# One kernel, a stack of eight gated attention and feed-forward blocks: TensorE's order, its PSUM banks and its idle stretches rearranged

## The chip, the cores and the metric

One core of a Trainium2 chip runs the whole program. The metric is the device time of one execution in microseconds, from the first to the last instruction and what lies around them; lower is better. TensorE (PE) multiplies, VectorE (DVE), ScalarE (ACT) and GpSimd (POOL) do the rest, SyncE (SP) issues the transfers.

## What is computed

The input is x of 64 batches x 64 tokens x 128 features and a context of 64 x 64 x 256. Eight blocks follow one another, each on a layer norm of x and each added to x with a gate:

```python
x = x + tanh(g_xattn[0]) * cross_attention(ctx, norm(x), masks)          # l0a: 8 heads of 16
x = x + tanh(g_ffn[0])   * two_layers(norm(x))                           # l0f0, l0f1: local attention, 8 heads of 64, and a gated MLP
x = x + tanh(g_xattn[1]) * (norm(x) @ W_in + b_in + patches of ctx)      # l1a
x = x + tanh(g_ffn[1])   * top2_of_8_experts(norm(x))                    # l1f
x = x + tanh(g_xattn[2]) * attention(norm(x), ctx, mask)                 # l2a: 8 heads of 16
x = x + tanh(g_ffn[2])   * ternary_mlp(norm(x))                          # l2f, l2g
x = x + tanh(g_xattn[3]) * attention(norm(x), [ctx, x])                  # l3a: 16 heads of 8, 128 keys, halves l3a0 and l3a1
x = x + tanh(g_ffn[3])   * ternary_conv_mlp(norm(x))                     # l3f, l3g
```

All of it is float32, with the masks and biases as bfloat16 rows that are multiplied by rows of ones (a value is split into three such rows).

## The kernel before

The 4,096 tokens are 32 tiles of 128 tokens (two batches). A tile goes through all eight blocks; nothing passes between tiles. Each engine runs one stream of instructions, written out by `in_turn`: every piece of work of a tile is a stage with a name (`l0f0_qk` is the multiplication for queries and keys in the first layer of block l0f), a table per engine gives each stage a time, tile i's stages are moved by i times `PERIOD`, and the engine's stream is all stages in order of that time. The numbers set nothing but the order. Five tiles (G = 5 sets of buffers) are under way at once, so each engine alternates between the stages of five tiles, and in the steady part the same sequence repeats once per tile: one turn of the sequence is called a period here.

Stages wait for one another with semaphores. In TensorE's chain `tile(name)` waits until stage `name` of the same tile is done (the operands), and `take(name)` waits until the readers of the PSUM banks that the stage writes are done with what stood there before. `BANK_TABLE` gives every TensorE stage its first bank, how many banks it takes, and which stage reads it last. TensorE works through its stream in order: whatever stands behind a waiting instruction waits too. Before, a stage first waits for its operands, then takes its banks, and then multiplies, masks and biases first:

```python
yield f"{n}_sc"                      # L1407
tile(f"{n}_qts")
take(f"{n}_sc")
...
mm(pair_of_banks(f"{n}_sc", 256)[:, h2], ident_bf[:], bc(causal[:], 1, 4), start=True, stop=False)
```

The stages of which the prediction speaks, in TensorE's stream: `l0f0_qk`, `l0f1_qk` (L1392, 128x512), `l0f0_v`, `l0f1_v` (L1398), `l0f0_qkt` and `l0f1_qkt` (L1405, eight transposes), `l0f0_sc` and `l0f1_sc` (L1412 the causal mask, L1418 the scores), `l1f_lg` (L1517, L1518), `l2a_yt` (a transpose, L1325), `l2a_sc` (L1346 and L1349 the mask and the logit bias, L1354 the scores), `l3a0_sc` and `l3a1_sc` (L1575), `l3f_hid` (L1619, the convolution; its start is used as the mark of a period). Around them: DVE's maximum and subtraction of a softmax (`_max` L1013, `_sub` L1016), its rotation of queries and keys (`_turned` L1067 and L1070) and their scaling (`_qkn` L1076), its `_y` (L997, the normalised tile), ACT's copies out of PSUM (L743), and POOL's powers (L507).

Of the kernel before, what the change touches and what calls it, by code (L numbers as in the profile page):

```python
# [42 lines left out]
PE_TIMES = """
    l0a_kv 711, l0a_yt 780, l0a_q 834, l0a_sc 855, l0a_pt 907, l0a_pv 914, l0a_ot 931, l0a_out 940, l0f0_yt 1016,
    l0f0_qk 1030, l0f0_v 1149, l0f0_qkt 1163, l0f0_sc 1163, l0f0_pt 1243, l0f0_pv 1303, l0f0_ot 1359, l0f0_wo 1379,
    l0f0_sh 1401, l0f0_lt 1465, l0f0_hid 1495, l0f0_out 1548, l0f1_yt 1573, l0f1_qk 1609, l0f1_v 1629,
    l0f1_qkt 1720, l0f1_sc 1819, l0f1_pt 1860, l0f1_pv 1879, l0f1_ot 1889, l0f1_wo 1897, l0f1_sh 1917, l0f1_lt 1977,
    l0f1_hid 1995, l0f1_out 2035, l1a_yt 2058, l1a_out 2065, l1f_yt 2102, l1f_lg 2102, l1f_ot 2188, l1f_out 2196,
    l2a_yt 2247, l2a_sc 2268, l2a_pt 2321, l2a_pv 2344, l2f_qt 2399, l2f_hid 2431, l2g_qt 2494, l2g_out 2520,
    l3a_yt 2539, l3a_qkv 2545, l3a0_sc 2564, l3a1_sc 2658, l3a0_pt 2693, l3a0_pv 2706, l3a1_pt 2712, l3a1_pv 2760,  # L50
    l3a_tt 2791, l3a_ot 2852, l3a_out 2863, l3f_qt 2896, l3f_hid 2941, l3g_qt 3022, l3g_out 3029
    """
# [12 lines left out]
DVE_TIMES = """
    l0a_st 652, l0a_var 667, l0a_eps 673, l0a_y 812, l0a_k 818, l0a_qs 838, l0a_max 868, l0a_sub 872, l0a_inv 947,
    l0a_o 953, l0a_x 973, l0f_st 976, l0f_var 990, l0f_eps 996, l0f_y 1000, l0f0_den 1105, l0f0_turned 1115,
    l0f0_qkn 1193, l0f0_max 1264, l0f0_sub 1286, l0f0_inv 1327, l0f0_o 1327, l0f0_y1 1385, l0f0_st 1405,
    l0f0_var 1425, l0f0_eps 1447, l0f0_y 1461, l0f0_gated 1526, l0f0_x 1571, l0f1_den 1695, l0f1_turned 1709,
    l0f1_qkn 1778, l0f1_max 1817, l0f1_sub 1839, l0f1_inv 1885, l0f1_o 1885, l0f1_y1 1943, l0f1_st 1951,  # L70
    l0f1_var 1951, l0f1_eps 1954, l0f1_y 1962, l0f1_gated 2039, l0f1_x 2054, l1a_st 2054, l1a_var 2054,
    l1a_eps 2068, l1a_y 2088, l1a_x 2106, l1f_st 2126, l1f_var 2127, l1f_eps 2139, l1f_lgs 2175, l1f_top 2196,
    l1f_mid 2202, l1f_rest 2218, l1f_sel 2218, l1f_w 2235, l1f_o 2248, l1f_x 2271, l2a_st 2278, l2a_var 2278,
    l2a_eps 2278, l2a_y 2278, l2a_max 2303, l2a_sub 2305, l2a_inv 2345, l2a_o 2362, l2a_x 2362, l2f_st 2362,
    l2f_var 2362, l2f_eps 2362, l2f_y 2362, l2f_abs 2377, l2f_lim 2411, l2f_inv 2419, l2f_step 2431, l2f_pre 2446,
    l2g_abs 2471, l2g_lim 2473, l2g_inv 2480, l2g_step 2480, l2g_x 2539, l3a_st 2539, l3a_var 2540, l3a_eps 2543,
    l3a_y 2550, l3a_part 2583, l3a0_max 2627, l3a0_sub 2644, l3a1_max 2752, l3a1_sub 2760, l3a_inv 2796, l3a_o 2821,
    l3a_x 2865, l3f_st 2865, l3f_var 2869, l3f_eps 2883, l3f_y 2883, l3f_abs 2908, l3f_lim 2910, l3f_inv 2917,
    l3f_step 2917, l3f_q 2923, l3f_act 2970, l3g_abs 2970, l3g_lim 2970, l3g_inv 3000, l3g_step 3024, l3f_x 3082
    """  # L80
# [1651 lines left out]
```

## Time and profile before

| | us |
|---|---|
| median of 3 runs | 1748.58 |
| lowest, highest | 1740.39, 1751.47 |
| the profiled execution, its own time | 1760.33 |
| its span | 1758.6 |
| TensorE busy | 1474.8 (84%) |
| VectorE busy | 1367.9 (78%) |
| ScalarE busy | 965.0 (55%) |
| GpSimd busy | 743.2 (42%) |
| mean granted TensorE clock | 0.911 of full |

Full TensorE clock is 2.4 GHz, granted clock 0.5 is 1.2 GHz. The share of an engine is a mean over a start, a steady part of some 1,335 us in which five tiles are under way, and an end in which the pipeline empties.

### The profile page before, as it was taken

Reading aid. Unit: us, or ns where it says so; the run is one execution under the profiler, and the core shown is the slowest. Engines: PE = TensorE matmul, PEld = TensorE weight load, DVE = VectorE, ACT = ScalarE, POOL = GpSimd, SP = SyncE. Lnnn points to the kernel's source line nnn. Section 1 sums busy time; section 2 is a strip of 40 time slices with the busy share of each in tenths; the row PEclk is TensorE's granted clock in tenths of the full one; section 3 lists DMA queues with packets and bytes.
Section 4 is the critical chain, followed back from the end, with each engine's and each line's share of the span. In section 5 each row is a group of like instructions: output and inputs, shape, how many; then the busy total and the mean of one; then the engine's idle time right before and its main releaser. Section 6 shows DMA issues by size and latency. Waiting matters only on the chain.

```text
span 1758.6 us, 42092 instructions
## 1 busy us (share of the span) xinstructions
PE 1474.8 (84%) x16270; PEld 1005.9 (57%) x16270; DVE 1367.9 (78%) x4054; ACT 965.0 (55%) x1992; POOL 743.2 (42%) x1143
## 2 busy tenths in 40 slices
PE   2567888899888889999888889998988889988764
PEld 1445565666566555666656566666566566665432
DVE  3356788887888888888888889888788888887652
ACT  1134565666566665666665565566555556565432
POOL 4244454433444554433544454444444554442200
PEclk9688899998999998999999999999899999998875
DMA  6001110111111110111111111011111110111100
GB/s 205 4 8 27 39 40 15 39 41 41 29 41 41 40 40 16 39 41 41 41 29 41 40 40 29 26 41 41 41 29 40 40 40 17 28 31 30 27 23 3
DMA packets 130948, 64.36 MB, mean 37 GB/s; under 512 B 97591, under 2 KB 123575, under 8 KB 130494
## 3 DMA queue, kind: packets, MB, share of 16 engines
q1 hardware_dynamic: 130750, 61.66, 13.5%
q8 instruction: 131, 2.15, 0.5%
q14 instruction: 67, 0.55, 0.1%
HBM read 50.05 MB, written 2.14 MB: 30 GB/s over the span
## 4 chain that ended last, share of the span: by engine, by line
PE 35%; DVE 35%; ACT 13%; POOL 8%; issue 7%; POOLq 2%; DVEq 0%
PE ps_all L1619 5%; DVE mx L1013 3%; POOL rden L507 3%; PE ps_all L1392 3%; PE ps_all L1575 3%; DVE wide_b L1016 3%; ACT wide_a L743 3%; DVE wide_b L1070 3%; POOL wide_a L507 3%; PE ps_all L1332 3%; DVE wide_a L1105 2%; DVE wide_a L1067 2%; PE ps_all L1418 2%; DVE den L1061 2%; DVE stats L982 2%
## 5 line engine op out<-in xcount | busy, mean ns | idle before, releaser
L507 POOL TENSOR_TENSOR rstd<-rstd,minus_half 128x1 f32<-128x1 f32 x320 | 177.1, 554 | 815.4 <-DVE rstd L991 815.4
L1013 DVE TENSOR_REDUCE mx<-ps_all 128x8 f32<-128x1024 f32 (+1 forms) x192 | 166.4, 867 | 133.0 <-PE ps_all L1354 96.6
L1332 PE MATMUL ps_all<-ident,wide_b 128*128 128x128 f32 x1024 | 173.8, 303 | 23.1 <-ACT wide_b L756 15.1
L507 POOL TENSOR_TENSOR rden<-rden,minus_half 128x16 f32<-128x16 f32 x64 | 187.6, 2931 | 9.4
L507 POOL TENSOR_TENSOR wide_a<-wide_a,wide_b 128x256 f32<-128x256 f32 x256 | 177.4, 725 | 0.0
L743 ACT COPY wide_a<-ps_all 128x512 f32<-128x512 f32 (+1 forms) x192 | 136.4, 729 | 61.3 <-PE ps_all L1332 36.9
L1332 PEld LDWEIGHTS ps_all<-ident,wide_b 128*128 128x128 f32 x1024 | 124.7, 153 | 53.2 <-ACT wide_b L756 18.4
L1392 PE MATMUL ps_all<-w_qkv,ht_shift 128*128 128x512 f32 x256 | 150.0, 717 | 2.2 <-ACT ht_shift L766 2.2
L743 ACT COPY ht<-ps_all 128x128 f32<-128x128 f32 x160 | 42.9, 268 | 193.1 <-PE ps_all L1325 193.0
L756 ACT ACTIVATE wide_b<-wide_b 128x512 f32<-128x512 f32 (+1 forms) x160 | 114.7, 717 | 44.2 <-DVE wide_b L1016 43.8
L743 ACT COPY wide_c<-ps_all 128x512 f32<-128x512 f32 (+1 forms) x96 | 69.9, 728 | 113.0 <-PE ps_all L1332 111.4
L1016 DVE TENSOR_TENSOR wide_b<-ps_all,mx 128x512 f32<-128x512 f32 (+1 forms) x160 | 125.8, 786 | 2.4
L706 ACT ACT_TABLE_LOAD x70 | 89.8, 1283 | 44.8 <-DVE wide_b L1016 19.4
L1575 PE MATMUL ps_all<-wide_a,qt 32*64 32x512 f32 x512 | 75.1, 668 | 40.0 <-DVE wide_a L1227 39.3
L1450 PE MATMUL ps_all<-ht,w 128*128 128x128 f32 x768 | 98.7, 282 | 1.3 <-ACT ht L741 1.3
L1450 PEld LDWEIGHTS ps_all<-ht,w 128*128 128x128 f32 x768 | 96.4, 201 | 1.8 <-issue 1.8
L1619 PE MATMUL ps_all<-w_conv,xt 128*64 128x512 f32 x384 | 95.1, 633 | 0.0
L1405 PEld LDWEIGHTS ps_all<-ident,wide_b 128*128 128x128 f32 x512 | 69.9, 161 | 40.3 <-issue 40.3
L1405 PE MATMUL ps_all<-ident,wide_b 128*128 128x128 f32 x512 | 78.2, 304 | 15.9 <-DVE wide_b L1076 14.2
L1392 PEld LDWEIGHTS ps_all<-w_qkv,ht_shift 128*128 128x128 f32 x256 | 49.7, 215 | 67.3 <-issue 67.3
L1076 DVE TENSOR_TENSOR wide_b<-wide_a,rden 128x1024 f32<-128x1024 f32 x64 | 77.8, 1215 | 11.3 <-POOL wide_c L675 8.5
L1061 DVE TENSOR_REDUCE den<-wide_c 128x16 f32<-128x1024 f32 x64 | 77.4, 1210 | 5.7 <-ACT wide_c L771 5.6
(267 smaller groups left out, 3714.5 us busy)
## 6 DMA issues: line engine op xcount, KB each, us to landing
wide_a<-in_k SPq DMA_DIRECT2D x64, 256.0 KB, 3.1
wide_c<-wide_c SPq DMA_DIRECT2D x128, 64.0 KB, 2.2
v_pad<-in_v SPq DMA_DIRECT2D x32, 256.0 KB, 3.8
v_pair<-in_v SPq DMA_DIRECT2D x32, 136.0 KB, 2.7
ctx_t<-in_ctx_t SPq DMA_DIRECT2D x32, 128.0 KB, 2.7
ctx_s<-in_ctx SPq DMA_DIRECT2D x32, 128.0 KB, 3.2
xin<-in_x SPq DMA_DIRECT2D x32, 64.0 KB, 2.6
mask_row<-in_mask_f SPq DMA_DIRECT2D x32, 64.0 KB, 3.0
```

The costliest lines, as they stand in the source:

```text
L507: return gp.tensor_tensor(o, a, b, op)
L743: a.copy(to, of).then_inc(*done(name))
L756: a.activation(of[:, s, 0:width], of[:, s, 0:width], ACT.Exp, scale=scale).then_inc(*done(f"{n}_exp"))
L1013: v.tensor_reduce(most, of, AX.X, ALU.max).then_inc(*done(f"{n}_max"))
L1016: tt(to, of, bc(most, 3, of.shape[3]), ALU.subtract).then_inc(*done(f"{n}_sub"))
L1061: v.tensor_reduce(den[:, s, :], wide_c[:, s, 0:2 * BANK].rearrange("p (g e) -> p g e", g=16), AX.X, ALU.add).then_inc(*done(f"{n}_den"))
L1332: m = nc.tensor.transpose(ps(name, c * P, P), of[:, c * P:c * P + P], ident[:])
L1392: m = mm(ps(f"{n}_qk", q * BANK, BANK), hs, w_qkv[:, L, q * INNER:q * INNER + INNER], start=True, stop=True)
L1405: m = nc.tensor.transpose(ps(f"{n}_qkt", c * P, P), wide_b[:, s, c * P:c * P + P], ident[:])
L1450: m = mm(ps(f"{n}_hid", half * BANK + c * P, P), w_1[:, L, half, c, :], ht[:, s, :], start=True, stop=True)
L1575: n_mm = mm(ps_all[64 * b:64 * b + 64, bank + m, :], qt[r, s, 64 * b:64 * b + 64], k_part[r, s, b * BANK:b * BANK + BANK], start=True, sto ...
L1619: m = mm(ps_all[64 * b:64 * b + 64, BANKS["l3f_hid"][0], :], xt[:, s, b, tap:tap + ROW], w_conv[:, tap, :], start=False, stop=(tap == 2))
```

## The change

Four things are changed, three of them on TensorE.

1. In every TensorE stage `take` comes ahead of the wait for operands, and where a stage begins with a mask or a bias, these multiplications come ahead of that wait too (`masks64` is split off from `scores64`; likewise the causal mask of `l0f0_sc` and `l0f1_sc`, and the biases of `l0f0_out`, `l0f1_out`, `l0a_kv`, `l1a_out`, `l3f_hid`).
2. After `take`, nine stages multiply the identity by itself into their own bank, one to three times, 16 times per tile (`WARM`); the stage then overwrites the result.
3. All tables of times and `PERIOD` have new numbers, that is, the streams of all engines are in a new order.
4. `BANK_TABLE` gives most stages other banks.

```diff
-PERIOD = 489
+PERIOD = 464
...
+WARM = {"l0a_yt": 2, "l0f0_qkt": 3, "l0f0_sc": 3, "l0f1_yt": 2, "l1a_yt": 1, "l1a_out": 1, "l1f_out": 1, "l3a_yt": 1, "l3a1_sc": 2}
...
 l0f0_sc 6 2 l0f0_sub
...
-l0f1_qk 6 2 l0f1_turned
+l0f1_qk 0 2 l0f1_turned
...
                         held[k] = [(reader, i) for reader in readers]
 
+                    for _ in range(WARM.get(name, 0)):
+                        mm(ps(name, 0, P), ident[:], ident[:], start=True, stop=True)
...
                     yield name
+                    take(name)
                     tile(wait)
-                    take(name)
                     nc.tensor.transpose(ps(name, 0, P), of, ident[:]).then_inc(*done(name))
...
                     yield f"{n}_sc"
-                    tile(f"{n}_qts")
                     take(f"{n}_sc")
                     settle(pe, "pe_waits")
                     for h2 in range(2):
                         mm(pair_of_banks(f"{n}_sc", 256)[:, h2], ident_bf[:], bc(causal[:], 1, 4), start=True, stop=False)
+                    tile(f"{n}_qts")
+                    settle(pe, "pe_waits")
...
                 yield "l2a_sc"
+                masks64("l2a", 1)
                 tile("l2a_ht")
                 pe.wait_ge(signal(f"second_in{s}"), loaded(i, 32))
-                take("l2a_sc")
-                settle(pe, "pe_waits")
-                scores64("l2a", ht[:, s, :], k_part[:, s, 0:BANK], 1)
+                scores64("l2a", ht[:, s, :], k_part[:, s, 0:BANK])
```

The first place is TensorE's stream around the queries and keys of the two layers of l0f, in the steady part. Before, in order: `l0f1_qk`, `l1f_yt`, `l1f_lg`, `l0f1_v` and `l0f0_v` (of two tiles), `l0f0_qkt`, `l0f0_sc`, `l3a1_sc`, and then the first stage of a new tile, `l0a_kv`:

```order
L1392 MATMUL ps_all<-w_qkv,ht_shift 128x512 x2
L1325 MATMUL ps_all<-ident,x 128x128
L1517 MATMUL ps_all<-w_gate,ht 128x8
L1518 MATMUL ps_all<-w_a,ht 128x128
L1398 MATMUL ps_all<-w_qkv,ht_shift 128x512 x2
L1405 MATMUL ps_all<-ident,wide_b 128x128 x8
L1412 MATMUL ps_all<-causal,ident_bf 128x256 x2
L1418 MATMUL ps_all<-wide_a 64x64 x16
L1575 MATMUL ps_all<-wide_a,qt 64x512 x4
L1465 MATMUL ps_all<-rows,row_sel 128x128
L1467 MATMUL ps_all<-w_src,ctx_t 128x128 x2
```

In the changed kernel the same stretch is `l0f1_qk`, `l1f_yt`, `l0f0_v`, `l1f_lg`, `l0f0_qkt`, `l0f0_sc`, `l3a1_sc`:

```order
L1403 MATMUL ps_all<-w_qkv,ht_shift 128x512 x2
L1329 MATMUL ps_all<-ident,x 128x128
L1409 MATMUL ps_all<-w_qkv,ht_shift 128x512
L1527 MATMUL ps_all<-w_gate,ht 128x8
L1528 MATMUL ps_all<-w_a,ht 128x128
L1319 MATMUL ps_all<-ident 128x128 x3
L1416 MATMUL ps_all<-ident,wide_b 128x128 x8
L1319 MATMUL ps_all<-ident 128x128 x3
L1422 MATMUL ps_all<-causal,ident_bf 128x256 x2
L1430 MATMUL ps_all<-wide_a 64x64 x16
L1319 MATMUL ps_all<-ident 128x128 x2
L1584 MATMUL ps_all<-wide_a,qt 64x512 x4
```

One of the two value multiplications stands ahead of `l1f_lg`, the other one has gone behind `l0a_kv` (its row is not in the piece); three identity multiplications stand ahead of the eight transposes, three ahead of the causal mask, and two ahead of `l3a1_sc`.

The second place is DVE's stream around the scores of l2a. Before, it is `l1f_x`, the statistics of l2a (L982, L985, L991), `l2a_y`, `l0a_y`, `l0a_k`, `l2a_max`, `l2a_sub`, `l0f0_inv`, `l0f0_o`, `l0a_qs`:

```order
L1190 TENSOR_TENSOR x<-ps_all,x 128x128
L982 BN_STATS stats<-x 128x6
L985 BN_AGGR mv<-stats 128x2
L991 TENSOR_SCALAR rstd<-mv 128x1
L997 TENSOR_SCALAR y<-x,mv,rstd 128x128
L997 TENSOR_SCALAR y<-xin,mv,rstd 128x128
L1132 SCALAR_TENSOR_TENSOR ot<-ps_all,b_k,mask_row 128x128
L1013 TENSOR_REDUCE mx<-ps_all 128x8
L1016 TENSOR_TENSOR wide_b<-ps_all,mx 128x512
L1024 RECIPROCAL rden<-ps_all 128x8
L1027 TENSOR_TENSOR wide_b<-ps_all,rden 128x2x4x64
L1136 SCALAR_TENSOR_TENSOR qt<-ps_all,b_q,mask_row 128x128
```

In the changed kernel the same names stand in this order, with all lines one further down in the file:

```order
L1191 TENSOR_TENSOR x<-ps_all,x 128x128
L983 BN_STATS stats<-x 128x6
L986 BN_AGGR mv<-stats 128x2
L992 TENSOR_SCALAR rstd<-mv 128x1
L1133 SCALAR_TENSOR_TENSOR ot<-ps_all,b_k,mask_row 128x128
L998 TENSOR_SCALAR y<-x,mv,rstd 128x128
L1137 SCALAR_TENSOR_TENSOR qt<-ps_all,b_q,mask_row 128x128
L1014 TENSOR_REDUCE mx<-ps_all 128x8
L1017 TENSOR_TENSOR wide_b<-ps_all,mx 128x512
L1014 TENSOR_REDUCE mx<-ps_all 128x8
L1017 TENSOR_TENSOR wide_b<-ps_all,mx 128x2x4x64
L1025 RECIPROCAL rden<-ps_all 128x8
```

`l0a_y` is gone from here (it stands some 20 stages earlier), `l0a_k` stands ahead of `l2a_y`, `l0a_qs` behind it and ahead of `l2a_max`, and `l0f1_max` and `l0f1_sub` follow at once on those of l2a.

The third piece is TensorE's stream at the same place. Before, four mask and bias rows follow `l0a_yt` and `l2a_yt`:

```order
L1325 MATMUL ps_all<-ident,y 128x128 x2
L1346 MATMUL ps_all<-rows,row_sel 128x256
L1349 MATMUL ps_all<-rows,row_sel 128x256
L1346 MATMUL ps_all<-rows,row_sel 128x256
L1349 MATMUL ps_all<-rows,row_sel 128x256
L1354 MATMUL ps_all<-wide_a,ht 64x256 x4
L1593 MATMUL ps_all<-wide_b,v_pad 32x64 x16
L1366 MATMUL ps_all<-wide_c,wide_a 64x65 x16
L1475 MATMUL ps_all<-ht,w_tgt 128x128
```

In the changed kernel only one transpose is left ahead of them, `l0a_q` stands between, and the scores of `l0f1_sc` follow before the values of l3a1 (L1602) and l0f0 (L1377):

```order
L1329 MATMUL ps_all<-ident,y 128x128
L1486 MATMUL ps_all<-ht,w_tgt 128x128
L1351 MATMUL ps_all<-rows,row_sel 128x256
L1354 MATMUL ps_all<-rows,row_sel 128x256
L1351 MATMUL ps_all<-rows,row_sel 128x256
L1354 MATMUL ps_all<-rows,row_sel 128x256
L1365 MATMUL ps_all<-wide_a,ht 64x256 x4
L1422 MATMUL ps_all<-causal,ident_bf 128x256 x2
L1430 MATMUL ps_all<-wide_a 64x64 x16
L1602 MATMUL ps_all<-wide_b,v_pad 32x64 x16
L1377 MATMUL ps_all<-wide_c,wide_a 64x65 x16
```

The order of the four mask rows and the scores is the same in both; what moved is the wait for `l2a_ht`, from ahead of the mask rows to behind them.

## Rows read from the trace of the kernel before

**Rows 1.** Windows: busy us (instructions) of each engine, granted clock, DMA share, GB/s.
```profile
core 0: us, PE busy (x) PEld busy (x) DVE busy (x) ACT busy (x) POOL busy (x), PEclk, DMA share, GB/s
0.00:229.40 229.40, 143.01 (x1379) 102.13 (x1379) 131.07 (x358) 76.78 (x159) 93.58 (x169) 0.85 0.19 54
229.40:1564.10 1334.70, 1196.59 (x13717) 822.34 (x13716) 1126.32 (x3376) 803.46 (x1675) 612.99 (x918) 0.94 0.14 36
1564.10:1758.60 194.50, 135.22 (x1176) 81.46 (x1175) 110.55 (x323) 84.78 (x160) 36.67 (x56) 0.77 0.08 22
```

**Rows 2.** The page's chain that ended last, shares of the span.
```profile
PE 35%; DVE 35%; ACT 13%; POOL 8%; issue 7%; POOLq 2%; DVEq 0%
```

**Rows 3.** Timeline of PE: the convolution, which marks a period (start, duration).
```profile
872.16 2.80 PE L1619 MATMUL ps_all<-w_conv,xt 128*64 128x512 f32 x12
...
919.48 2.79 PE L1619 MATMUL ps_all<-w_conv,xt 128*64 128x512 f32 x12
...
969.12 2.79 PE L1619 MATMUL ps_all<-w_conv,xt 128*64 128x512 f32 x12
```

**Rows 4.** Windows of two successive periods, columns as in rows 1.
```profile
871.50:918.82 47.32, 41.90 (x510) 28.94 (x509) 41.64 (x126) 29.84 (x62) 22.67 (x34) 1.00 0.14 38
918.82:968.46 49.64, 44.57 (x510) 31.45 (x509) 41.65 (x126) 29.72 (x62) 22.68 (x34) 0.93 0.15 36
```

**Rows 5.** Timeline of PE in a full-clock stretch: start, us, what, [idle before <-releaser].
```profile
887.29 1.09 PE L1575 MATMUL ps_all<-wide_a,qt 32*64 32x512 f32 x8 [1.32 <-DVE wide_a L1227]
...
891.06 0.36 PE L1517 MATMUL ps_all<-w_gate,ht 128*128 128x8 f32 x2 [0.66 <-DVE wide_b L1016]
...
891.58 1.88 PE L1398 MATMUL ps_all<-w_qkv,ht_shift 128*128 128x512 f32 x4
893.30 1.04 PE L1405 MATMUL ps_all<-ident,wide_b 128*128 128x128 f32 x8
895.81 0.38 PE L1412 MATMUL ps_all<-causal,ident_bf 128*128 128x256 bf16 x2 [1.47 <-DVE wide_b L1070]
896.12 0.69 PE L1418 MATMUL ps_all<-wide_a 64*64 64x64 f32 x32
896.74 1.09 PE L1575 MATMUL ps_all<-wide_a,qt 32*64 32x512 f32 x8
...
899.77 1.09 PE L1332 MATMUL ps_all<-ident,wide_b 128*128 128x128 f32 x8
```

**Rows 6.** Timeline of PE one period on, at half clock.
```profile
948.62 1.91 PE L1332 MATMUL ps_all<-ident,wide_b 128*128 128x128 f32 x8
```

**Rows 7.** Timelines of DVE and ACT beside rows 5.
```profile
890.84 1.22 DVE L1076 TENSOR_TENSOR wide_b<-wide_a,rden 128x1024 f32<-128x1024 f32 x1
...
894.38 1.01 ACT L743 COPY wide_a<-ps_all 128x1024 f32<-128x1024 f32 x1 [0.28 <-PE ps_all L1405]
...
894.43 1.27 DVE L1070 TENSOR_TENSOR wide_b<-ps_all,turn 128x512 f32<-128x512 f32 x2
```

**Rows 8.** Timeline of DVE around the scores of l2a.
```profile
901.90 0.28 DVE L1190 TENSOR_TENSOR x<-ps_all,x 128x128 f32<-128x128 f32 x1
...
903.58 0.35 DVE L997 TENSOR_SCALAR y<-x,mv,rstd 128x128 f32<-128x128 f32 x1 [0.67 <-POOL rstd L507]
...
904.10 0.35 DVE L1132 SCALAR_TENSOR_TENSOR ot<-ps_all,b_k,mask_row 128x128 f32<-128x128 f32 x1
906.33 0.69 DVE L1013 TENSOR_REDUCE mx<-ps_all 128x8 f32<-128x512 f32 x1 [1.89 <-PE ps_all L1354]
```

**Rows 9.** Timeline of PE at the same place.
```profile
903.40 1.06 PE L1332 MATMUL ps_all<-ident,wide_a 128*128 128x128 f32 x8
904.32 0.41 PE L1325 MATMUL ps_all<-ident,y 128*128 128x128 f32 x2
905.08 0.27 PE L1346 MATMUL ps_all<-rows,row_sel 128*128 128x256 bf16 x1 [0.35 <-ACT ht L741]
...
905.60 0.66 PE L1354 MATMUL ps_all<-wide_a,ht 64*64 64x256 f32 x8
```

**Rows 10.** Timeline of PE: six 128x128 float32 multiplications (12 records) and what follows.
```profile
922.37 1.50 PE L1450 MATMUL ps_all<-ht,w 128*128 128x128 f32 x12
923.71 0.27 PE L1325 MATMUL ps_all<-ident,y 128*128 128x128 f32 x1
```

More of the change, by code:

```diff
@@ L39 @@
 BIASES = 1408
-PERIOD = 489
+PERIOD = 464
 PE_TIMES = """
[L44 to L51, printed above, removed]
+    l0a_kv 180, l0a_yt 211, l0a_q 253, l0a_sc 300, l0a_pt 375, l0a_pv 378, l0a_ot 394, l0a_out 395, l0f0_yt 470,
+    l0f0_qk 494, l0f0_v 601, l0f0_qkt 625, l0f0_sc 625, l0f0_pt 699, l0f0_pv 725, l0f0_ot 810, l0f0_wo 833,
+    l0f0_sh 841, l0f0_lt 870, l0f0_hid 931, l0f0_out 985, l0f1_yt 986, l0f1_qk 1061, l0f1_v 1123, l0f1_qkt 1158,
+    l0f1_sc 1183, l0f1_pt 1257, l0f1_pv 1287, l0f1_ot 1304, l0f1_wo 1314, l0f1_sh 1329, l0f1_lt 1358, l0f1_hid 1407,
+    l0f1_out 1449, l1a_yt 1477, l1a_out 1489, l1f_yt 1526, l1f_lg 1544, l1f_ot 1595, l1f_out 1614, l2a_yt 1632,
+    l2a_sc 1646, l2a_pt 1682, l2a_pv 1695, l2f_qt 1787, l2f_hid 1810, l2g_qt 1876, l2g_out 1906, l3a_yt 1941,
+    l3a_qkv 1944, l3a0_sc 1977, l3a1_sc 2019, l3a0_pt 2063, l3a0_pv 2079, l3a1_pt 2092, l3a1_pv 2114, l3a_tt 2122,
+    l3a_ot 2179, l3a_out 2189, l3f_qt 2259, l3f_hid 2285, l3g_qt 2380, l3g_out 2409
@@ L76 @@
[L76 to L79, printed above, removed]
+    l0a_st 89, l0a_var 105, l0a_eps 135, l0a_y 168, l0a_k 282, l0a_qs 284, l0a_max 315, l0a_sub 322, l0a_inv 361,
@@ L96 @@
     """
 BANK_TABLE = """
-l0a_kv 3 1 l0a_k
+l0a_kv 0 1 l0a_k
 l0a_yt 7 1 l0a_ht
-l0a_q 4 1 l0a_qs
-l0a_sc 0 2 l0a_sub
-l0a_pt 1 1 l0a_pts
-l0a_pv 4 2 l0a_o
+l0a_q 3 1 l0a_qs
+l0a_sc 2 2 l0a_sub
+l0a_pt 7 1 l0a_pts
+l0a_pv 5 2 l0a_o
 l0a_ot 1 1 l0a_ots
-l0a_out 5 1 l0a_x
+l0a_out 3 1 l0a_x
 l0f0_yt 5 1 l0f0_hs
-l0f0_qk 4 2 l0f0_turned
-l0f0_v 0 1 l0f0_vs
-l0f0_qkt 1 2 l0f0_qts
+l0f0_qk 3 2 l0f0_turned
+l0f0_v 7 1 l0f0_vs
+l0f0_qkt 3 2 l0f0_qts
 l0f0_sc 6 2 l0f0_sub
-l0f0_pt 2 1 l0f0_pts
-l0f0_pv 1 2 l0f0_o
@@ L128 @@
-l0f1_sh 0 1 l0f1_y
-l0f1_lt 4 1 l0f1_lts
-l0f1_hid 1 2 l0f1_gated
-l0f1_out 6 1 l0f1_x
-l1a_yt 0 1 l1a_ht
-l1a_out 1 1 l1a_x
-l1f_yt 2 1 l1f_ht
-l1f_lg 4 1 l1f_o
-l1f_ot 4 1 l1f_ots
-l1f_out 0 1 l1f_x
-l2a_yt 4 1 l2a_ht
-l2a_sc 5 2 l2a_sub
-l2a_pt 5 1 l2a_pts
-l2a_pv 6 2 l2a_o
-l2f_qt 5 1 l2f_qts
-l2f_hid 2 1 l2f_pre
-l2g_qt 0 1 l2g_qts
-l2g_out 7 1 l2g_x
-l3a_yt 3 1 l3a_ht
-l3a_qkv 6 2 l3a_part l3a_vs
+l0f1_sc 2 2 l0f1_sub
+l0f1_pt 0 1 l0f1_pts
+l0f1_pv 2 2 l0f1_o
+l0f1_ot 1 1 l0f1_ots
+l0f1_wo 7 1 l0f1_y1
@@ L148 @@
+l0f1_sh 4 1 l0f1_y
+l0f1_lt 4 1 l0f1_lts
+l0f1_hid 0 2 l0f1_gated
+l0f1_out 7 1 l0f1_x
+l1a_yt 5 1 l1a_ht
+l1a_out 6 1 l1a_x
+l1f_yt 6 1 l1f_ht
+l1f_lg 5 1 l1f_o
+l1f_ot 5 1 l1f_ots
+l1f_out 6 1 l1f_x
+l2a_yt 7 1 l2a_ht
+l2a_sc 4 2 l2a_sub
+l2a_pt 4 1 l2a_pts
+l2a_pv 5 2 l2a_o
+l2f_qt 5 1 l2f_qts
+l2f_hid 7 1 l2f_pre
+l2g_qt 2 1 l2g_qts
+l2g_out 6 1 l2g_x
+l3a_yt 7 1 l3a_ht
+l3a_qkv 0 2 l3a_part l3a_vs
 l3a0_sc 3 2 l3a0_sub
-l3a1_sc 1 2 l3a1_sub
-l3a0_pt 6 2 l3a0_pts
-l3a0_pv 0 1 l3a0_os
+l3a1_sc 2 2 l3a1_sub
@@ L1384, in layer @@
                     yield f"{n}_qk"
+                    take(f"{n}_qk")
                     tile(f"{n}_hs")
@@ L1423, in layer @@
                     yield f"{n}_pv"
+                    take(f"{n}_pv")
                     tile(f"{n}_pts")
@@ L1514, in chain @@
                 yield "l1f_lg"
+                take("l1f_lg")
                 tile("l1f_ht")
-                take("l1f_lg")
                 mm(ps("l1f_lg", P, E), ht[:, s, :], w_gate[:], start=True, stop=True)
```

154 lines of the change are left out of this document (78 added, 76 removed).

## The prediction, made blind

> **What bounds the kernel now.** I read the windows first. In the steady part TensorE is busy 1196.6 of 1334.7 us and DVE 1126.3, no other engine over 804, at a mean granted clock of 0.94 [rows 1]; the chain of work that ended last lies on PE and DVE for 35% each [rows 2]. So neither alone is the bound: each waits for the other at some places, and the length of a period is what counts. From 229.4 to 1564.1 us there are 27 periods, marked by the start of the convolution: 1334.7 / 27 = 49.43 us each.
>
> Then the marks themselves. The period that starts at 872.16 lasts 47.32 us, the next one 49.64 [rows 3]. Their work is the same, 510 PE records and DVE 41.6 us in both, but the first one has full clock (1.00, 2.4 GHz) and PE busy 41.90, the second one 0.93 and 44.57 [rows 4]. The half clock of 1.2 GHz doubles what it touches: eight transposes take 1.09 us at full clock and 1.91 at half [rows 5, 6]. So the 2.67 us that PE loses to the clock in the second period show in the period as 2.32. A mean period is 49.43 - 47.32 = 2.11 us longer than one at full clock, 57 us over 27 periods. I take this as the first thing that the change can win.
>
> Where does the clock fall? Ahead of both places PE is idle or in short pieces. In the full-clock stretch PE waits 1.32 us ahead of `l3a0_sc`, 0.66 ahead of `l1f_lg`, 1.47 ahead of `l0f0_sc` [rows 5]; one period later the same sequence is at half clock some 4 us behind that last wait [rows 6]. In all PE is idle 47.32 - 41.90 = 5.42 us of a full-clock period, DVE 47.32 - 41.64 = 5.68 [rows 4].
>
> The Trainium skill ("TensorE: Matmul & The Clock Gate", Part 1) says that for modelling the warm-up costs less than 1% of a typical kernel span, which would be under 18 us here. The trace disagrees: 2.11 of 49.43 us is 4.3%, because the clock falls again in nearly every period. The measurement decides.
>
> **The identity multiplications.** They are 16 per tile. The nearest row is six float32 multiplications of the same size, from 922.37 to 923.71: 1.34 / 6 = 0.223 us each at full clock [rows 10]. So 16 x 0.223 = 3.6 us per period, 7.1 if all ran at half clock. The trace before shows none, so from both sides: at best they lie wholly in PE's idle time and lift the clock for good, which is worth 2.11 us; at worst they lie on the path and lift nothing, which costs 3.6 to 4. PE's own floor becomes 41.9 + 3.6 = 45.5 us. They stand at just the places named: five in the stages ahead of `l3a0_sc` (`l0f1_yt`, `l3a_yt`, `l1a_yt`, `l1a_out`), eight from `l0f0_qkt` to `l3a1_sc`, three close behind. I take it that they win back four fifths of the 2.11, and leave 0.4: they turn idle time into activity right ahead of the points where the clock fell, but PE will still wait somewhere.
>
> The skill's page on TensorE ("TensorE: Matmul & The Clock Gate", Part 4) says that transposes do not engage the full clock as multiplications do. The two stretches ahead of the falls do hold many transposes, and the added ones are plain multiplications; no row here separates the two kinds. It would change my 0.4 to about 0.
>
> **The order and the masks, at full clock.** First place, the queries and keys of l0f0. DVE has scaled them at 890.84 + 1.22 = 892.06 [rows 7], but PE gets to the transposes only at 893.30, behind `l1f_lg` and two value multiplications in 1.88 us [rows 5]. With one of the two gone from there (1.88 / 2, near 0.9), PE is free near 891.6; three identities (0.67) take it to 892.3. The transposes start 1.0 us earlier. ACT's copy (1.01 us, 894.38 before [rows 7]) then ends near 894.4. Before, the scores also waited for banks 6 and 7, which DVE read for the other layer until 894.43 + 1.27 = 895.70 [rows 7]; `l0f1_qk` now has banks 0 and 1, so that wait goes. Three identities and the causal mask (0.67 + 0.3) lie beside ACT's copy. The scores start near 894.4 against 896.12 [rows 5], 1.7 us earlier. What is late next is DVE: it has the 41.6 us to do, runs without a gap here, and the maximum of these scores still stands behind the rotation of the other layer. So at this place PE gains 1.7 us less the 0.45 of the two identities ahead of `l3a1_sc`, and the path gains nothing by itself; the gain is that PE is early at the next place.
>
> Second place, the scores of l2a. Here DVE is the one that waits: `l1f_x` at 901.90, 0.67 us of idle for POOL's power, `l2a_y` at 903.58, `l0a_k` at 904.10, and then 1.89 us idle until the scores of l2a let it start at 906.33 [rows 8]. On PE that chain is: `l2a_yt` at 904.32, held up by eight transposes of l3a1 until then, 0.35 us for ACT's copy, four mask rows from 905.08 to 905.60, scores from 905.60 [rows 9]. After the change PE arrives here about 1 us earlier, so the transpose can follow `l2a_y` (near 903.95), the copy ends near 904.6, and the masks (905.60 - 905.08 = 0.52 us) lie inside the wait for it. Scores start near 904.65, and DVE near 905.35: 1.0 us sooner. DVE moreover does `l0a_qs` (an operation like the 0.35 of `l0a_k`) inside what is left of the 1.89, work that had stood behind it. Against that, `l0a_y` (another 0.35) has left this stretch, where it cost nothing, for the dense part ahead of `l1f_x`. `l0a_k` was beside the wait and still is. Sum at this place: 1.0 + 0.35 - 0.35 = 1.0 us.
>
> The mask rows of the other stages, the biases ahead of their operands and the extra semaphore pieces (three more per tile) I cost at nothing: they lie beside waits for operands that PE has there anyway, and the semaphores beside the multiplications still under way. If that cover is not there, each mask row that the path loses or keeps is 0.13 us (0.52 / 4 [rows 9]), a few tenths in all, either way. The other reordering, ACT's and POOL's too, I cannot price from rows; both have room (29.8 and 22.7 busy of 47.3 [rows 4]). Bounds: nothing from below, and from above all of DVE's idle time, to its floor of 41.6. I take nothing.
>
> So at full clock: by DVE's path 47.32 - 1.0 = 46.3; by PE, 45.5 of work and some wait that nothing fills, half of the 1.32 ahead of `l3a0_sc` at least, 46.2. I take 46.3, plus 0.4 for what is left of the slow clock: **46.7 us a period.**
>
> **The sum.** 27 x (49.43 - 46.7) = 73.7 us. The start and the end (229.4 and 194.5 us at clocks of 0.85 and 0.77 [rows 1]) have far more idle time than the steady part; more clock there, at 0 to 15 us, of which I take 5, as the waits are longer than one to three multiplications can bridge. That is 78.7 us off the profiled execution's own 1760.33, 1681.6. The median of the runs shown lies 11.75 below it, 1748.58, so **1670 us**.
>
> **Rivals.**
> - *PE becomes the bound, and the clock is whole* (10%). All waits fill, the period is 45.6: 27 x 3.83 + 8 = 111 us less, 1637. For it: every other engine has 4 us to spare. Against: PE and DVE take turns, and neither was ever without waits.
> - *Half of the clock's loss stays* (18%). Whether it falls depends on where the waits come, and the new order has its own. 46.3 + 1.05 = 47.35: 56 + 4 us less, 1689; with less from the order up to 1725.
> - *The identities do not do what they are for* (12%). PE's busy time was 1196.6 / 27 = 44.3 us per period, slow time included. With 16 x 0.25 more (0.25, as an eighth of the time is at half clock, 1 - 0.94 = 0.06, twice) it is 48.3; add 1 us of waits and it is 49.3, no better than 49.43: 1742.
> - *Slower* (8%): the eight identities from `l0f0_qkt` to `l3a1_sc` stand ahead of operands that are there already. This decides itself at one point: if PE reaches `l0f0_qkt` later than DVE's 892.06 plus the time of three identities, each one is on the path. Before, PE was 1.2 us late there. With the clock unchanged, 8 x 0.25 = 2.0 less the 1.0 of the second place, 1.0 x 32 = 32 us more: 1781. Against it: with 0.9 us of value work and the 1.47 us wait gone, it has the time.
>
> **How the numbers follow.** My forecast of 46.7, give or take 0.6 (1654 to 1686), has 52%. Faster by over 1% (below 1731) are the forecast and the first two: 80%. Within 1%, about what this measurement can tell, 12%; slower by over 1%, 8%. The range goes from the first rival's 1637 to the third one's 1742, and leaves out the slower case and a little at either end.
>
> **What would show it.** Marks of the convolution 46 to 47.5 us apart; granted clock of the steady part 0.98 or more against 0.94; PE busy near 45.5 us a period; DVE's wait at L1014 for l2a under 1.0 us against 1.89; the wait ahead of the causal mask gone. Wrong it is if the clock stays at 0.94 (then the identities do not count), or if the clock is whole but the period stays at 47.3 or more (then the order gave nothing, or the identities stand on the path; DVE's idle time would tell).

## The result, and the profile after

The changed kernel takes 1685.4 us (median of 4, 1683.4 to 1686.0), the kernel before beside it on the same chip 1750.0: a ratio of 0.964, 95% interval 0.960 to 0.968. The forecast was 1670 and faster; it is faster, inside the range, and the gain is 65 us where 79 were forecast. Of the two profiled executions, from which the forecast was worked out, the gain is 75.1 us: 1760.33 against 1685.26.

The windows of the changed kernel, with the same columns as [rows 1], give two successive periods and the whole steady part, from the first mark (the convolution, now L1628) to the 28th:

```profile
794.15:841.23 47.08, 44.66 (x542) 32.75 (x543) 41.62 (x126) 29.98 (x63) 23.00 (x34) 1.00 0.15 38
841.23:888.31 47.08, 44.66 (x542) 32.74 (x542) 41.61 (x126) 29.97 (x63) 23.00 (x34) 1.00 0.15 38
222.40:1502.40 1280.00, 1207.36 (x14555) 885.33 (x14582) 1125.86 (x3376) 809.48 (x1675) 620.83 (x918) 1.00 0.15 37
```

Against [rows 1] and [rows 4]: the granted clock is 1.00 in the whole steady part, not 0.94. TensorE is busy 44.7 us of a full-clock period instead of 41.9, with 32 more records (16 float32 multiplications of two each). 27 periods last 1280.0 us, 47.41 each, where they were 49.43; 14 of them last 47.1, the longest four 48.1 to 49.2. The start is 7.0 us shorter (222.4 against 229.4) and what lies behind the 28th mark 13.3 (1683.5 - 1502.4 = 181.1 against 194.4). So the 75.1 us of the two profiled spans are 54.7 in the steady part and 20.4 at the ends.

The chain that ended last has changed hands, to be set beside [rows 2]; POOL was 8% and is now 24%:

```profile
PE 25%; POOL 24%; DVE 20%; issue 11%; ACT 9%; POOLq 7%; SPq 2%; DMA 0%; DVEq 0%
```

TensorE's timeline at the first place, which answers to [rows 5]:

```profile
809.11 1.09 PE L1584 MATMUL ps_all<-wide_a,qt 32*64 32x512 f32 x8 [0.44 <-DVE wide_a L1228]
...
813.37 0.83 PE L1319 MATMUL ps_all<-ident 128*128 128x128 f32 x6
814.03 1.05 PE L1416 MATMUL ps_all<-ident,wide_b 128*128 128x128 f32 x8
814.92 0.83 PE L1319 MATMUL ps_all<-ident 128*128 128x128 f32 x6
815.59 0.38 PE L1422 MATMUL ps_all<-causal,ident_bf 128*128 128x256 bf16 x2
816.28 0.69 PE L1430 MATMUL ps_all<-wide_a 64*64 64x64 f32 x32 [0.31 <-ACT wide_a L744]
```

The waits of 1.32, 0.66 and 1.47 us are now 0.44, none and 0.31. From the start of `l3a0_sc` to that of the scores of `l0f0_sc` it is 7.17 us (816.28 - 809.11); before it was 8.83 (896.12 - 887.29). That is the 1.7 us of the forecast, identities and all.

DVE's and POOL's timelines at the second place answer to [rows 8]; ahead of them stands the mark from which this period is counted:

```profile
794.10 2.79 PE L1628 MATMUL ps_all<-w_conv,xt 128*64 128x512 f32 x12
```

```profile
823.54 0.28 DVE L1191 TENSOR_TENSOR x<-ps_all,x 128x128 f32<-128x128 f32 x1
...
825.87 0.63 DVE L998 TENSOR_SCALAR y<-x,mv,rstd 128x128 f32<-128x128 f32 x1 [1.05 <-POOL rstd L508]
827.20 0.35 DVE L1137 SCALAR_TENSOR_TENSOR qt<-ps_all,b_q,mask_row 128x128 f32<-128x128 f32 x1 [0.71 <-PE ps_all L1486]
828.26 0.69 DVE L1014 TENSOR_REDUCE mx<-ps_all 128x8 f32<-128x512 f32 x1 [0.71 <-PE ps_all L1365]
```

```profile
822.42 1.61 POOL L508 TENSOR_TENSOR ctx_rms<-ctx_rms,minus_half 128x1 f32<-128x1 f32 x1
824.22 0.59 POOL L618 TENSOR_SCALAR far<-plug,patch_row,ctx_rms 128x64 f32<-128x64 f32 x1 [0.18 <-issue]
824.80 0.51 POOL L620 TENSOR_SCALAR far<-plug,patch_row 128x64 f32<-128x64 f32 x1
825.27 0.57 POOL L508 TENSOR_TENSOR rstd<-rstd,minus_half 128x1 f32<-128x1 f32 x1
```

The wait of 1.89 us for the scores has become 0.71 and 0.71, with `l0a_qs` between. But the wait ahead of `l2a_y` has grown from 0.67 to 1.05: POOL's power for it starts at 825.27, behind `pick_reach` of a later tile (L508 `ctx_rms`, L618, L620). From `l1f_x` to `l2a_y` it is 2.33 us now and was 1.68; from `l2a_y` to the maximum 2.39 and was 2.75. In sum DVE gets to the maximum of l2a no sooner: it starts 34.16 us behind the mark of its period (828.26 - 794.10), and before it was 34.17 (906.33 - 872.16). The 0.24 us by which the clean period has become shorter lie behind this maximum, where `l0a_qs` (0.35 us) no longer stands.

### The profile page after: what moved, and what is told of

Its sections match the earlier page's. It is cut to its first block, busy times and chain, and to the rows that moved or that the text cites. A ratio compares the mean times of both kernels' runs of the same rounds, so it can differ in the third digit from the quotient of the medians.

```text
span 1683.5 us, 44176 instructions
## 1 busy us (share of the span) xinstructions
PE 1484.5 (88%) x17261; PEld 1079.7 (64%) x17294; DVE 1366.6 (81%) x4054; ACT 971.6 (58%) x1992; POOL 751.7 (45%) x1143
## 4 chain that ended last, share of the span: by engine, by line
PE 25%; POOL 24%; DVE 20%; issue 11%; ACT 9%; POOLq 7%; SPq 2%; DMA 0%; DVEq 0%
POOL rden L508 9%; POOL wide_a L508 9%; POOL rstd L508 4%; PE ps_all L1336 4%; POOLq L617 3%; POOLq L615 3%; PE ps_all L1377 3%; DVE wide_a L1106 3%; PE ps_all L1329 2%; PE ps_all L1448 2%; ACT L707 2%; PE ps_all L1365 2%; DVE small L1041 2%; DVE y L998 2%; ACT wide_b L788 2%
## 5 line engine op out<-in xcount | busy, mean ns | idle before, releaser
L508 POOL TENSOR_TENSOR rstd<-rstd,minus_half 128x1 f32<-128x1 f32 x320 | 179.0, 565 | 750.7 <-DVE rstd L992 750.6
L508 POOL TENSOR_TENSOR rden<-rden,minus_half 128x16 f32<-128x16 f32 x64 | 187.6, 2931 | 9.4
L508 POOL TENSOR_TENSOR wide_a<-wide_a,wide_b 128x256 f32<-128x256 f32 x256 | 177.6, 724 | 0.0
L1319 PE MATMUL ps_all<-ident 128*128 128x128 f32 x1024 | 167.3, 285 | 7.0 <-DVE wide_b L1017 3.9
L1336 PE MATMUL ps_all<-ident,wide_b 128*128 128x128 f32 x1024 | 149.8, 280 | 26.2 <-ACT wide_b L757 13.0
L744 ACT COPY wide_a<-ps_all 128x512 f32<-128x512 f32 (+1 forms) x192 | 139.7, 729 | 41.1 <-PE ps_all L1336 21.9
L1336 PEld LDWEIGHTS ps_all<-ident,wide_b 128*128 128x128 f32 x1024 | 117.6, 143 | 52.3 <-ACT ht L744 28.6
L1319 PEld LDWEIGHTS ps_all<-ident 128*128 128x128 f32 x1024 | 140.9, 196 | 14.0 <-DVE wide_b L1017 6.3
L1403 PE MATMUL ps_all<-w_qkv,ht_shift 128*128 128x512 f32 x256 | 125.7, 614 | 2.2 <-ACT ht_shift L767 2.2
L1628 PE MATMUL ps_all<-w_conv,xt 128*64 128x512 f32 x384 | 93.4, 623 | 0.4 <-ACT xt L744 0.4
L998 DVE TENSOR_SCALAR y<-x,mv,rstd 128x128 f32<-128x128 f32 x128 | 57.2, 447 | 35.9 <-POOL rstd L508 35.9
L1416 PE MATMUL ps_all<-ident,wide_b 128*128 128x128 f32 x512 | 71.1, 284 | 14.5 <-DVE wide_b L1077 14.5
```

The costliest lines, as they stand in the source:

```text
L508: return gp.tensor_tensor(o, a, b, op)
L744: a.copy(to, of).then_inc(*done(name))
L998: ts(y[:, s, :], x[:, s, :] if of is None else of, mv[:, s, 0:1], rstd[:, s:s + 1], ALU.subtract, ALU.mult).then_inc(*done(f"{n}_y"))
L1319: mm(ps(name, 0, P), ident[:], ident[:], start=True, stop=True)
L1336: m = nc.tensor.transpose(ps(name, c * P, P), of[:, c * P:c * P + P], ident[:])
L1403: m = mm(ps(f"{n}_qk", q * BANK, BANK), hs, w_qkv[:, L, q * INNER:q * INNER + INNER], start=True, stop=True)
```

## The experiments

The runs were timed in three groups, each on one chip beside the kernel before, which had 1750.2, 1753.8 and 1749.6 us in them. The mean period is that over 27 periods between the marks, the clean period the one that most periods of that kernel have at full clock, slow time that at 1.2 GHz per steady period. Periods, clocks and slow times are those of one profiled execution of each kernel. The kernel before has only three periods at full clock, all of 47.32, and old_order_new_waits six.

| kernel | median us | ratio (95%) | mean period | clean period | slow time |
|---|---|---|---|---|---|
| before | | 1 | 49.43 | 47.32 | 5.7 |
| changed | 1685.4 | 0.964 (0.960 to 0.968) | 47.41 | 47.08 | 0 |
| no_warm | 1692.9 | 0.967 (0.962 to 0.971) | 47.61 | 47.07 | 1.5 |
| old_order_new_waits | 1746.6 | 0.997 (0.993 to 1.001) | 49.51 | 47.39 | 5.8 |
| old_order_new_waits_warm | 1731.6 | 0.988 (0.984 to 0.993) | 48.88 | 48.87 | 0 |
| late_masks | 1691.7 | 0.966 (0.962 to 0.970) | 47.59 | 47.50 | 0 |
| new_order_old_waits | 1715.5 | 0.979 (0.976 to 0.982) | 48.16 | 47.52 | 1.1 |
| new_order_old_banks | 2013.9 | 1.149 (1.145 to 1.153) | 58.02 | | 10.2 |
| warm_transposes | 1681.8 | 0.960 (0.958 to 0.962) | 47.40 | 47.08 | 0 |
| pick_moved | 1666.6 | 0.951 (0.948 to 0.954) | 46.86 | 46.55 | 0 |
| dup_first | 1681.7 | 0.960 (0.957 to 0.964) | 47.29 | 47.07 | 0 |
| all_three | 1660.7 | 0.949 (0.946 to 0.952) | 46.71 | 46.42 | 0.1 |
| old_order_transposes | 1706.2 | 0.974 (0.971 to 0.978) | 48.08 | 48.05 | 0 |
| warm_twice | 1717.2 | 0.981 (0.978 to 0.984) | 48.51 | 48.39 | 0 |

**1. The changed kernel without the identities (no_warm).** Theory A, the forecast's, was that they hold up the clock and that this is the gain.

```diff
-WARM = {"l0a_yt": 2, "l0f0_qkt": 3, "l0f0_sc": 3, "l0f1_yt": 2, "l1a_yt": 1, "l1a_out": 1, "l1f_out": 1, "l3a_yt": 1, "l3a1_sc": 2}
+WARM = {}
```

> The changed kernel without its 16 identity multiplications per tile; all else as changed. Theory A (the gain is the clock, and the identities hold it up): the granted clock of the steady part falls back to 0.94 to 0.96, the period grows from 47.4 to 49 or more, 1735 to 1750 us. Rival B (the new order alone has closed the waits, and the identities are ballast on TensorE): the clock stays at 0.98 or more, TensorE has 2.8 us less to do per period, 1665 to 1685 us.

Measured 1692.9 us, 7.5 above the changed kernel, with intervals of the ratio that overlap. Neither expectation was met whole: the time is near Rival B's, but the clock does fall. Two neighbouring periods of it, in the columns of [rows 1]:

```profile
696.10:744.10 48.00, 42.49 (x508) 30.16 (x508) 41.70 (x126) 29.90 (x63) 23.01 (x34) 0.96 0.15 37
744.10:791.20 47.10, 41.13 (x510) 29.06 (x510) 41.64 (x126) 29.96 (x63) 23.01 (x34) 1.00 0.15 38
```

In 12 of the 27 periods the clock falls once and costs mostly some 0.9 us; slow time is 1.5 us a period against 5.7 before. So the new order without any identity already keeps most of the clock, and theory A falls in its size. TensorE is less busy than before (41.13), idle nearly 6 us of 47.1, and its clock still falls less often. So the amount of idle time does not decide it. What differs is how the idle time lies: the longest waits of the clean period are below one microsecond, where [rows 5] has 1.32 and 1.47. That this is the reason is read from the traces; no run changed the length of a wait alone.

```profile
756.15 0.33 PE L1329 MATMUL ps_all<-ident,y 128*128 128x128 f32 x1 [0.85 <-DVE y L998]
759.12 1.09 PE L1584 MATMUL ps_all<-wide_a,qt 32*64 32x512 f32 x8 [0.72 <-DVE wide_a L1228]
...
766.24 0.70 PE L1430 MATMUL ps_all<-wide_a 64*64 64x64 f32 x32 [0.97 <-ACT wide_a L744]
```

**2. Old order and banks, new waits (old_order_new_waits).** The changed kernel's code, with `PERIOD`, the tables of times and `BANK_TABLE` of the kernel before, and `WARM = {}`.

> The kernel before with its own order and banks, but with banks taken and masks and biases multiplied ahead of the operands' wait; no identities. Theory A: the clock stays near 0.94 in the steady part, and the masks alone are worth at most 0.5 us a period: 1735 to 1752 us. Rival B (the masks ahead of the wait fill the idle stretches and so lift the clock): clock 0.97 or more, 1700 us or less.

Measured 1746.6 us, not to be told from the kernel before. Theory A's expectation holds: taking banks and multiplying masks and biases ahead of the wait brings nothing that the times show in the old order (its ten runs go from 1730.6 to 1759.6 us, and its full-clock periods are 47.39 us against 47.32).

**3. The same with the identities (old_order_new_waits_warm).** Only `WARM` is put back.

> The same with the 16 identities per tile: old order and banks, new waits, identities. Theory A: the clock goes to 1.00 in the steady part and the period to 47 to 48 us, 1685 to 1710 us, so that nearly the whole gain is there without the new tables. Rival C (order and banks bring a good part): 1715 to 1745 us, either because the identities lie on the path in the old order or because the clock still falls.

Measured 1731.6 us, which is Rival C's. The clock is 1.00 in the steady part, as theory A said, but nearly every period is 48.87 us, 1.55 longer than the 47.32 of a full-clock period before and 1.48 longer than the 47.39 of run 2, the same kernel without identities. The timeline shows where a part of that is:

```profile
1028.04 1.04 PE L1416 MATMUL ps_all<-ident,wide_b 128*128 128x128 f32 x8
1029.90 0.94 PE L1319 MATMUL ps_all<-ident 128*128 128x128 f32 x6 [0.82 <-DVE wide_b L1071]
1030.67 0.38 PE L1422 MATMUL ps_all<-causal,ident_bf 128*128 128x256 bf16 x2
1030.98 0.69 PE L1430 MATMUL ps_all<-wide_a 64*64 64x64 f32 x32
```

The identities write the stage's own banks, so they too wait until DVE's L1071 (the rotation of the other layer) has left banks 6 and 7. Only then do three identities run, and they push the scores back. In the changed kernel's row for the same three there is no wait: `l0f1_qk` is in other banks.

**4. Old order, identities as transposes (old_order_transposes).** A transpose of the identity is one record, not two.

```diff
-                        mm(ps(name, 0, P), ident[:], ident[:], start=True, stop=True)
+                        nc.tensor.transpose(ps(name, 0, P), ident[:], ident[:])
```

> Old order and banks, new waits, the 16 identities as transposes (half the records each). Theory L (in the old order the identities hold the clock but lie on the path, which is why the period is 48.87 us at full clock against 47.32 without them): about half of the 1.55 us goes, period 48.0 to 48.3 us, 1700 to 1715 us, clock 1.00 in the steady part. Rival M (the 1.55 us is not the identities' own time but banks taken earlier): period stays 48.7 or more, 1726 to 1735 us.

Measured 1706.2 us, period 48.05, clock 1.00: theory L. TensorE has about 1.9 us less to do per period than in run 3 (43.60 against 45.48) and the period is 0.82 shorter, so in the old order a good part of the identities' own time is on the path. The waits of 1.32 and 1.47 us of [rows 5] are still there with 1.17 and 1.16 us, and TensorE is idle 4.5 us of a period, yet the clock does not fall.

**5. New order, old waits (new_order_old_waits).** The kernel before with `PERIOD`, all tables and `BANK_TABLE` of the changed one; operands are awaited first, no identities.

> The code of the kernel before with the tables of the changed one: new order and banks, but operands awaited first, masks behind the wait, no identities. Theory E (order and banks do most; the masks are worth 0.2 to 0.5 us a period): 1695 to 1715 us, period 47.6 to 48.3 us, granted clock of the steady part 0.96 to 0.98. Rival F (the new waits are needed for the new order to pay, since they fill the idle stretch ahead of the scores): 1720 us or more, with slow time back at 4 us a period or more.

Measured 1715.5 us, half a microsecond above theory E's range, with the period (48.16) inside it and the clock (0.99) above it: 0.979 of before from the tables alone. TensorE is busy 41.16 of a clean period of 47.5 us and waits 1.2 us ahead of the causal mask, but slow time is 1.1 us a period against 5.7. Set beside run 1 (1692.9), the new waits are worth 22 us in the new order, where they showed nothing in the old one: mean period 48.16 against 47.61, clean period 47.52 against 47.07.

**6. Changed kernel, masks late again (late_masks).**

```diff
                     take(f"{n}_sc")
+                    tile(f"{n}_qts")
                     settle(pe, "pe_waits")
                     for h2 in range(2):
                         mm(pair_of_banks(f"{n}_sc", 256)[:, h2], ident_bf[:], bc(causal[:], 1, 4), start=True, stop=False)
-                    tile(f"{n}_qts")
-                    settle(pe, "pe_waits")
```

and likewise for the masks of l0a and l2a and the five biases.

> The changed kernel, but masks and biases are multiplied behind the wait for the operands again (banks are still taken first and the identities still stand ahead of the wait). Theory A (the masks are worth the 0.52 us of the four rows of l2a at DVE's longest wait, and little elsewhere): 0.3 to 0.7 us a period, 10 to 22 us slower than the changed kernel, 1695 to 1708 us. Rival D (they lie beside other waits; POOL's power sets the time at that place): within 5 us of it, 1680 to 1690 us.

The medians, 1691.7 and 1685.4, are of runs timed apart, and their ratios' intervals overlap; the periods of the traces are clearer: 47.50 clean against 47.08. That is 0.42 us, inside theory A's 0.3 to 0.7, and near the 0.45 that run 5 shows, so in a clean period the masks are what the new waits bring. The time is some 3 us short of what theory A gave, and Rival D's 1690 is missed by 2. The mean period is only 0.18 us longer (47.59 against 47.41), because this trace has fewer of the long periods of run 11; the 22 us of run 5 are therefore not shown to be the masks' alone.

**7. New order, old banks (new_order_old_banks).** Run 1 with the old `BANK_TABLE`.

> New order and new waits without identities, but the old table of banks. Theory E1 (the order carries the gain): within 10 us of the 1692.9 us of the changed kernel without identities. Rival E2 (the banks carry it: the layers' queries and keys no longer share banks 6 and 7 with the scores): 1720 us or more, with a wait of 1 us or more ahead of the causal mask again.

Measured 2013.9 us. The wait that Rival E2 named is there, 3.4 us in each of the seven periods looked at:

```profile
PE ps_all L1422 <- DVE wide_b L1071: 24.0, 7, 3.4
PE ps_all L1422 <- DVE wide_b L1017: 11.4, 7, 1.6
PE ps_all L1329 <- DVE wide_b L1017: 10.0, 7, 1.4
```

(total us, times, longest). But the old banks were laid out for another order, and several stages wait; the run shows that the new order needs the new banks (the new banks under the old order were not tried), and says nothing on which of them carries the gain of run 5.

**8. Transposes in the new order (warm_transposes).** The edit of run 4 in the changed kernel.

> The changed kernel with the 16 identity multiplications as transposes of the identity. If only multiplications hold the clock up: about 1.5 us of slow time per period, as without any (1692.9 us), 1690 to 1700 us. If transposes count like multiplications: no slow time in the steady part, 1680 to 1687 us.

Measured 1681.8 us and no slow time in the steady part: the second expectation. The clock is held by transposes as by multiplications. All four executions agree: the granted clock over the whole of one is 0.966 to 0.971, and 0.950 to 0.956 in the four of run 1.

**9. Twice the identities (warm_twice).** `range(2 * WARM.get(name, 0))`.

> The changed kernel with 32 identities per tile instead of 16. TensorE is busy 44.7 us of a full-clock period of 47.08 and would be busy 47.5 with them all. Theory N (in the new order the 16 lie beside waits at almost no price, and TensorE has 2.4 us of room): the period goes to 48.0 to 49.0 us, 1715 to 1745 us, bound by TensorE. Rival O (even the first 16 lie on the path, one for one): 47.08 + 2.8 to 3.6 = 49.9 to 50.7 us, 1775 us or more.

Measured 1717.2 us, clean period 48.39, theory N:

```profile
902.50:950.90 48.40, 47.53 (x572) 36.24 (x572) 41.78 (x126) 29.84 (x63) 22.85 (x34) 1.00 0.16 37
```

TensorE is busy 47.53 of 48.4 us. The first 16 cost 44.66 - 41.13 = 3.53 us of its time (0.22 each) and 0.01 us of the clean period, the second 16 cost 1.31 us of the period. Here TensorE is busy 98% of the period and is the bound; with 16 it isn't.

**10. One stage moved on POOL (pick_moved).** What then makes the 47.08? The profile after names the 1.05 us wait.

```diff
-    pick_reach 293, picks 1017
+    pick_reach 267, picks 1017
```

> The changed kernel with one stage moved on GpSimd: pick_reach (3.2 us, of a later tile) goes from just ahead of the power of l2a into the 2.9 us in which GpSimd waits for the sums of l0f1. Theory G (that stage holds up the power for which DVE waits 1.05 us ahead of l2a_y, and with it the period of 47.07 us): period 46.3 to 46.8 us, 1660 to 1678 us. Rival H (another wait takes its place at once, or the 0.3 us that it now overhangs the sums of l0f1 costs the same): within 5 us of 1685.

Measured 1666.6 us, clean period 46.55: theory G, inside both of its ranges. DVE now waits 0.41 us, POOL waits for DVE, and the maximum of l2a starts 33.63 us behind its period's mark (at 831.76), the same 0.53 sooner than in the changed kernel by which the period is shorter:

```profile
862.88 0.63 DVE L998 TENSOR_SCALAR y<-x,mv,rstd 128x128 f32<-128x128 f32 x1 [0.41 <-POOL rstd L508]
865.39 0.69 DVE L1014 TENSOR_REDUCE mx<-ps_all 128x8 f32<-128x512 f32 x1 [0.71 <-PE ps_all L1365]
```

```profile
862.30 0.55 POOL L508 TENSOR_TENSOR rstd<-rstd,minus_half 128x1 f32<-128x1 f32 x1 [2.49 <-DVE rstd L992]
```

**11. One stage moved on SP (dup_first).** A few periods of the changed kernel are 48 to 49 us long. They hold a wait at the values of l0f0 (L1377) or just ahead of them (L1602).

```diff
-    l0a_dup 0, l0f0_dup 342, l0f1_dup 719, second 1107, first 1167, third 1532, store 2313
+    l0a_dup 0, l0f0_dup 252, l0f1_dup 719, second 1107, first 1167, third 1532, store 2313
```

> The changed kernel with one stage moved on SP: the copy of the values of l0f0 (l0f0_dup) is issued ahead of that of l0f1, whose source is ready some 8 us later. Theory J (the periods of 48 to 49 us among those of 47.08 are waits of l0f0_pv, L1377, for this copy): all steady periods 47.1 us, mean 47.1 to 47.2 against 47.41, 1673 to 1680 us. Rival K (they have another cause, or it is hidden by the next wait): long periods stay, within 5 us of 1685.

Measured 1681.7 us, mean period 47.29, with three periods of 48.4 to 48.6 left. Theory J mostly falls: the copy now starts 9 us earlier and the long periods are still there. Their waits are put down to nothing that the profile shows ("issue"), as in the period from 361 us, where the chain of work stops between the 31st and the 32nd of one stage's 32 multiplications, inside one multiplication of the code, where there is no wait:

```profile
396.22 0.58 PE ps_all L1602 x31
396.80 0.95 issue
397.74 0.22 PE ps_all L1602
```

The traces show more of it than these rows. The stop comes at the same instruction whatever the kernel does elsewhere: behind the 7,100th and the 16,052nd record of TensorE (multiplications and weight loads counted together) in the changed kernel, in dup_first and in pick_moved, 0.9 to 1.3 us each time. All stops over 0.5 us inside such a group in these three traces lie whole multiples of 255.8 records apart (13, 35 or 39 such lengths from one to the next), and so do those of warm_transposes, whose stream has other numbers. Transfers of 16,384 bytes on the queue that the profile calls `instruction` start once in some 254 such records, and one starts 1.3 to 2.0 us ahead of each of these stops. So they keep to places in TensorE's own stream, which speaks for the loading of its instructions and against a semaphore. This is read from traces and no run tries it. The four stops of the changed kernel lie in its four longest periods, which hold 5.5 of the 8.9 us that its 27 periods have above 47.08. In all, what lies above the clean period is worth 0.2 to 0.3 us in the mean period.

**12. The three together (all_three).** `pick_reach` moved, `l0f0_dup` first, identities as transposes.

> The changed kernel with pick_reach moved, l0f0_dup first, and the identities as transposes. If the three add up: full-clock period 46.55 throughout, 0.3 us under the mean of 46.86 with pick_reach alone, and a few us from the cheaper transposes: 1650 to 1660 us, faster than both kernels. If one of them only opens the way to the next wait: 1662 to 1668 us.

Measured 1660.7 us, just above the first range, 0.949 of before: the fastest kernel of the study, 25 us below the changed one. The interval of its ratio overlaps that of pick_moved alone, so of the three only `pick_reach` is clearly shown to matter. One of its periods was 49.5 us long with the clock down once, which no clean trace of the 16 multiplications shows; one such period is no evidence on either side.

## Why the prediction was right, and where it was not

- *TensorE loses its clock, and that is worth 2.11 us a period: right.* The changed kernel gets all of it back, where 0.4 was to be left; in its place 0.33 us lie between the mean and the clean period, for the most part in the four periods with the stops of run 11. The half clock does not quite "double" what it touches: the eight transposes of [rows 5] and [rows 6] take 1.75 times as long.
- *The identities are what brings it back: wrong as to who.* The step that failed is "I take it that they win back four fifths of the 2.11". Order, banks and waits alone cut the slow time from 5.7 to 1.5 us a period (run 1); the identities clear the rest, 0.20 us of the mean period, which is no more than the long periods of run 11 differ from trace to trace. That the clock came out whole as forecast is in this part luck. In the old order they do clear all 5.8 (run 3 against run 2), but take about 1.5 us of the path for it. The parts in their own order: tables 49.43 to 48.16, new waits to 47.61, identities to 47.41.
- *Their price is 0.223 us each, TensorE's work 45.5 us: right to 1% for each,* 3.53 / 16 = 0.22. The work is 44.7, since without them it had fallen to 41.1.
- *They stand beside waits and not on the path: right for this order and these banks* (0.01 us of the clean period in run 1 against the changed kernel); in the old ones it does not hold (runs 3 and 4). The slower rival named the mechanism, but another point: not operands that were there already, but a bank that was still held.
- *First place, 1.7 us earlier on TensorE: right,* 8.83 to 7.17.
- *Second place, 1.0 us of DVE's path: wrong.* This is the term that was mis-sized: the clean period went from 47.32 to 47.08, 0.24, and the maximum of l2a starts no sooner in it (34.16 us behind the mark, 34.17 before). From `l2a_y` to the maximum it is 2.39 us, with `l0a_qs` inside; before it was 2.75, and the forecast's times give 1.8. The `l2a_y` itself takes 0.63 us where the forecast had the 0.35 of before. And `l2a_y` comes 0.65 us later behind `l1f_x`, because the step "The other reordering, ACT's and POOL's too, I cannot price from rows; both have room" let POOL pass because of its mean load. POOL's own order had put 3.2 us of another tile ahead of the power that DVE waits for; run 10 moves it away and gets 0.53 us back, a clean period of 46.55. That is near the 46.3 forecast for full clock, but of a kernel with one more change than the forecast knew.
- *The ends, 5 us: too little, 20.4 measured.* Most of it is not the identities' work: without them (run 1) the start is 220.1 us and the end 184.4, against 229.4 and 194.5 before and 222.4 and 181.1 in the changed kernel. The steady part won 54.7 where 73.7 were forecast. The two errors nearly cancel, 19.0 against 15.4, which is luck: 75.1 us between the profiled executions where 78.7 were forecast.
- *The step from the profiled execution to the median, 11.75 us: this is most of the distance between 1670 and 1685.* The profiled execution of the kernel before was a long one, and the forecast took the same 11.75 us off the changed kernel. The times of the kernel before go with its clock (1742.6 us at 0.925, 1757.0 at 0.914 in the runs beside run 1); the changed kernel's four lie within 2.6 us, and its profiled one at the median.
- *A slip in the sums:* the third rival's 1742 does not follow from its 49.3 us a period; 27 x 0.13 = 3.5 us, which gives 1745. It changes nothing.
- *The Trainium skill's sentence on the warm-up's cost* ("TensorE: Matmul & The Clock Gate", Part 1) was set against 4.3% of a period. It speaks of the warm-up that a kernel pays as it starts, and here the clock fell again and again, so the trace does not contradict it; it was the wrong sentence for this kernel. Getting the clock back in the old order with the cheaper transposes gave 2.6% of the whole time (run 4).
- *The Trainium skill's sentence on transposes* ("TensorE: Matmul & The Clock Gate", Part 4), of which the forecast said that it would change 0.4 to about 0, is not borne out: transposes of the identity, among the multiplications of this kernel, hold the clock at 1.00 in runs 4 and 8.
